# Stack loads with 4 KB rows, and the residual image in an SBUF ring of four

## The reference, cut to what matters

```python
x = x + _L0_conv_ref(_gn(x), ...)      # gn, router, shared conv, 2 expert convs, group norms, silu
x = x + _L1_conv_ref(_gn(x), ...)      # window attention on the result
# inside _L1_conv_ref
qkv = einsum('oc,bchw->bohw', qkv_w, x) + qkv_b
scores = einsum('bhnd,bhmd->bhnm', q, k) / sqrt(HD) + bias
o = einsum('bhnm,bhmd->bhnd', softmax(scores), v)
pe = depthwise_conv7x7(v_img)
out = einsum('oc,bchw->bohw', proj_w, x_img + pe) + proj_b
```

## Time and profile before

| | |
|---|---|
| median of 3 runs | 871.91 us |
| the profiled execution: its time | 872.17 us |
| the profiled execution: its span | 870.4 us |
| PE busy | 674.7 us, 78% |
| DVE busy | 601.1 us, 69% |
| ACT busy | 450.8 us, 52% |
| moved by DMA | 145.29 MB |
| one step of the loop in its middle | 40.9 us |

### The profile page before, as it was taken

The page is one execution under the profiler, slowest core; times in us unless marked ns, Lnnn a source line. Parts: engine busy times, 40 slices in busy tenths (PEclk is TensorE's granted clock), DMA queues, the critical chain, the costliest instruction groups (busy, mean ns, idle before and its releaser), DMA issues.

```text
span 870.4 us, 18688 instructions
## 1 busy us (share of the span) xinstructions
PE 674.7 (78%) x6926; PEld 409.1 (47%) x6926; DVE 601.1 (69%) x1136; ACT 450.8 (52%) x746; POOL 185.9 (21%) x289
## 2 busy tenths in 40 slices
PE   5225829696979788797979697979796969788785
PEld 4212315464646454555545454646463647444321
DVE  4734456778778787869687777777777888532396
ACT  1114445565657474746565556656565655354321
POOL 3122042222223130404130312222221011000044
PEclk9987759697989898989989897979797979999999
DMA  8232553948575664759594939394956345587345
GB/s 344 105 120 67 178 149 94 197 120 203 131 188 152 168 191 142 189 156 192 142 208 137 219 102 220 110 215 123 209 128 167 108 130 156 183 275 248 121 183 203
DMA packets 92751, 145.29 MB, mean 167 GB/s; under 512 B 24691, under 2 KB 65782, under 8 KB 92662
## 3 DMA queue, kind: packets, MB, share of 16 engines
q1 hardware_dynamic: 66806, 100.90, 41.1%
q0 software_dynamic: 21248, 25.36, 14.3%
q10 hardware_dynamic: 4608, 17.86, 5.6%
HBM read 84.21 MB, written 51.41 MB: 156 GB/s over the span
## 4 chain that ended last, share of the span: by engine, by line
PE 50%; DVE 20%; issue 12%; DMA 11%; ACT 3%; POOL 2%; POOLq 1%; SPq 1%; DVEq 0%; ACTq 0%
PE g L1069 14%; PE g L1087 5%; PE g L1065 5%; PE pv L1152 4%; PE t L1137 4%; DVE xr L840 4%; PE s L1126 3%; DMA vt<-x 3%; PE s L1259 3%; DMA xs<-xn 3%; PE g L1170 2%; PE t L1259 2%; PE g L1097 2%; PE s L1122 2%; DMA xsh<-xs 2%
## 5 line engine op out<-in xcount | busy, mean ns | idle before, releaser
L525 ACT ACTIVATE y<-g 128x512 f32<-128x512 f32 x96 | 57.1, 597 | 192.2 <-PE g L1065 104.4
L1069 PE MATMUL g<-xsh,wsel 96*128 96x512 f32 x256 | 132.1, 645 | 16.1 <-DMA xsh<-xs 15.4
L810 DVE BATCH_NORM_STATS2 st<-y 128x6 f32<-128x512 f32 x96 | 66.3, 692 | 99.1 <-ACT y L525 99.1
L874 DVE TENSOR_REDUCE mx<-s 128x8 f32<-128x512 f32 x128 | 87.2, 681 | 28.6 <-PE s L1126 27.9
L878 DVE TENSOR_TENSOR less<-s,mx 128x512 f32<-128x512 f32 x128 | 88.5, 692 | 4.4
L1122 PE MATMUL s<-bias,ident 128*128 128x512 f16 x128 | 51.1, 399 | 51.7 <-DMA stack<-sk_d 51.7
L1137 PE MATMUL t<-ident,less 128*128 128x128 f32 x512 | 79.4, 278 | 15.1 <-ACT pt L596 15.1
L596 ACT ACTIVATE pt<-t 128x512 f32<-128x512 f32 x128 | 74.7, 596 | 24.6 <-PE t L1137 18.0
L1137 PEld LDWEIGHTS t<-ident,less 128*128 128x128 f32 x512 | 62.4, 145 | 49.8 <-issue 36.9
L1152 PE MATMUL pv<-vp,pt 128*64 128x34 f32 x2048 | 82.8, 227 | 3.0 <-DVE ot L892 2.6
L1069 PEld LDWEIGHTS g<-xsh,wsel 96*128 96x128 f32 x256 | 49.5, 207 | 72.8 <-issue 54.0
(11 more groups left out here) (159 smaller groups left out, 1176.5 us busy)
## 6 DMA issues: line engine op xcount, KB each, us to landing
xsh<-xs POOLq DMA_DIRECT2D x64, 210.0 KB, 7.3
stack<-sq_d SPq DMA_DIRECT2D x96, 128.0 KB, 5.2
stack<-sk_d SPq DMA_DIRECT2D x192, 64.0 KB, 5.2
xs<-xn ACTq DMA_DIRECT2D x16, 578.0 KB, 3.3
vt<-x SPq DMA_DIRECT2D x4, 2048.0 KB, 18.3
xin<-x POOLq DMA_DIRECT2D x16, 512.0 KB, 7.8
acc_d<-xr SPq DMA_DIRECT2D x16, 512.0 KB, 5.1
sq_d<-qhl SPq DMA_DIRECT2D x32, 256.0 KB, 2.1
```

The lines of the kernel that those rows point to most:

```text
L525: act.activation(y[:, k, h * HALF:(h + 1) * HALF], g[at][:, :], ACT.Identity).then_inc(g_free[at], 1)
L810: last = v.bn_stats(st[:, 2 * k + h, :], y[:, k, h * HALF:(h + 1) * HALF])
L874: v.tensor_reduce(mx[:, p % 2, :], scored, AX.X, ALU.max).then_inc(sem["s_max"], 1)
L1069: last = mm(g[at][:, :], wsel[:, k - 1, C * dy:C * dy + C], xsh[:, k - 1, dy + 16 * h:dy + 16 * h + 16, 0:W], start=(dy == 0), stop=(dy == 1))
```

## The change

The DRAM copies of q and k are laid out by half, then high and low, and the channels of q and k are permuted on the host so that the four channels that one partition takes are neighbours: one row of 4 KB. The loads of a half go from 3 + 6 to 4 + 4: for each parity one of 16 partitions (`high_rows`) and one of 32 partitions that takes high and low together (`both_rows`). The tiles `qs` and `ks` get the same order, as does the score matmul. The single `xr` and `x1` become `xr` with four slots; the projection is added in the slot; save_xr and load_x1 go; save_acc and load_acc stay for the first 12 images, and the last four never leave SBUF. `l1s` moves into `vn`.

```diff
-STACK = 16 * 9
+STACK = 16 * 8
+KEEP = 4
-        xr = sb("xr", [C, PIX])
-        x1 = sb("x1", [C, PIX])
+        xr = sb("xr", [C, KEEP, PIX])
-        acc = free[0:B]
+        acc = free[0:B - KEEP] + [xr[:, n, :] for n in range(KEEP)]
-        sq_d = nc.dram_tensor("sq_d", [2, C, PIX], F16).ap()
+        sq_d = nc.dram_tensor("sq_d", [2, 2, C, HALF], F16).ap()
+            def high_rows(src, half, a):
+                return src[half, 0].rearrange("(a c i) n -> a c (i n)", a=2, i=Q)[a]
+
+            def both_rows(src, half, a):
+                size = C * HALF
+                return bass.AP(src.tensor, 2 * half * size + a * size // 2, [[size, 2], [Q * HALF, HD], [1, Q * HALF]])
...
-                for part, t in enumerate((0, 1, 0)):
-                    sp.dma_start(qs[QD * part:QD * part + QD, :, cols],
-                                 sq_d[t, :, cols].rearrange("(i c) n -> c i n", i=Q)).then_inc(stacked[half], 16)
+                for a in range(2):
+                    dst = qs[3 * HD * a:3 * HD * (a + 1), half, :, :].rearrange("p i n -> p (i n)")
+                    sp.dma_start(dst[0:HD], high_rows(sq_d, half, a)).then_inc(stacked[half], 16)
+                    sp.dma_start(dst[HD:3 * HD], both_rows(sq_d, half, a)).then_inc(stacked[half], 16)
...
-                for part, t in enumerate((0, 0, 1)):
-                    for par in range(2):
-                        rows = QD * part + HD * par
-                        src = sk_d[t, :, cols].rearrange("(i a c) n -> a c i n", i=Q, a=2)
-                        sp.dma_start(ks[rows:rows + HD, :, par, cols], src[par]).then_inc(stacked[half], 16)
+                for a in range(2):
+                    dst = ks[3 * HD * a:3 * HD * (a + 1), half, a, :, :].rearrange("p i n -> p (i n)")
+                    sp.dma_start(dst[0:2 * HD], both_rows(sk_d, half, a)).then_inc(stacked[half], 16)
+                    sp.dma_start(dst[2 * HD:3 * HD], high_rows(sk_d, half, a)).then_inc(stacked[half], 16)
...
             def step(b, has1, has2, has3):
-                if b:
-                    load_x1(b - 1)
...
-                if b:
+                if 0 < b <= B - KEEP:
                     save_acc(b - 1)
...
-                if has2:
-                    save_xr(b + 2)
...
                 if c == 1:
-                    act.wait_ge(sem["acc_saved"], 16 * B)
+                    act.wait_ge(sem["acc_saved"], 16 * (B - KEEP))
+                    for h in range(2):
+                        wait_emptied(act, "pr", B - 1, h)
-                if c:
+                if 0 < c <= B - KEEP:
                     load_acc(c - 1)
...
                 if part == 0:
-                    if j:
-                        dve.wait_ge(sem["xr_saved"], 16 * j)
-                        dve.wait_ge(sem["xw_done"], j)
+                    if j >= KEEP:
+                        dve.wait_ge(sem["acc_saved"], 16 * (j - KEEP + 1))
```

More of the change, by code:

```diff
@@ L151, in program @@
         stack = sb("stack", [C, 3 * Q * PIX // 2])
-        qs = stack[:, 0:Q * PIX // 2].bitcast(F16).rearrange("p (i n) -> p i n", i=Q)
-        ks = stack[:, Q * PIX // 2:].bitcast(F16).rearrange("p (i a n) -> p i a n", i=Q, a=2)
+        qs = stack[:, 0:Q * PIX // 2].bitcast(F16).rearrange("p (h i n) -> p h i n", h=2, i=Q)
+        ks = stack[:, Q * PIX // 2:].bitcast(F16).rearrange("p (h a i n) -> p h a i n", h=2, a=2, i=Q)
         TAPS = 2 * 2 * DWK * QD
@@ L193, in program @@
         ri = sb("ri", [B, 8], U32)
-        l1s = sb("l1s", [3, C])
+        l1s = vn[0:3, 0:C]
         hb = o[:, 0:TABLE]
-        free = [y[:, n, :] for n in range(3)] + [xin[:, 0, :], xin[:, 1, :], xr[:, :], x1[:, :], xw[:, :], o[:, :]]
+        free = [y[:, n, :] for n in range(3)] + [xin[:, 0, :], xin[:, 1, :], xw[:, :], o[:, :]]
         free += [t[:, :, :].rearrange("p t n -> p (t n)").bitcast(F32) for t in (qhl, khl)]
@@ L261, in save_half @@
                     sp.wait_ge(stacked[half], STACK * j)
-                sp.dma_start(dst.rearrange("t c n -> c t n")[:, :, cols], src[:, :, cols]).then_inc(saved[half], 16)
+                sp.dma_start(dst[half].rearrange("t c n -> c t n"), src[:, :, cols]).then_inc(saved[half], 16)
             def save_q(j):
@@ L331, in save_acc @@
                     wait_emptied(sp, "pr", b, h)
-                sp.dma_start(image_acc(b), x1[:, :]).then_inc(sem["acc_saved"], 16)
+                sp.dma_start(acc_d[b], xr[:, b % KEEP, :]).then_inc(sem["acc_saved"], 16)
             def step(b, has1, has2, has3):
-                if b:
-                    load_x1(b - 1)
                 if has1:
@@ L834, in residual @@
                 wk = [route[:, j, k:k + 1] for k in range(TOP)]
+                kept = xr[:, j % KEEP, :]
                 if part == 0:
                     dve.wait_ge(sem["silu_done"], 3 * j + 1)
-                    if j:
-                        dve.wait_ge(sem["xr_saved"], 16 * j)
-                        dve.wait_ge(sem["xw_done"], j)
-                    v.tensor_tensor(xr[:, :], y[:, 0, :], xin[:, j % 2, :], ALU.add).then_inc(sem["sum_shared"], 1)
+                    if j >= KEEP:
+                        dve.wait_ge(sem["acc_saved"], 16 * (j - KEEP + 1))
+                    v.tensor_tensor(kept, y[:, 0, :], xin[:, j % 2, :], ALU.add).then_inc(sem["sum_shared"], 1)
                     return
@@ L844, in residual @@
                     dve.wait_ge(sem["sum_shared"], j + 1)
-                    v.scalar_tensor_tensor(out=xr[:, :], in0=y[:, 1, :], scalar=wk[0], in1=xr[:, :],
+                    v.scalar_tensor_tensor(out=kept, in0=y[:, 1, :], scalar=wk[0], in1=kept,
                                            op0=ALU.mult, op1=ALU.add).then_inc(sem["sum_first"], 1)
@@ L849, in residual @@
                 dve.wait_ge(sem["sum_first"], j + 1)
-                v.scalar_tensor_tensor(out=xr[:, :], in0=y[:, 2, :], scalar=wk[1], in1=xr[:, :],
+                v.scalar_tensor_tensor(out=kept, in0=y[:, 2, :], scalar=wk[1], in1=kept,
                                        op0=ALU.mult, op1=ALU.add).then_inc(sem["xr_done"], 1)
@@ L853, in residual @@
                 for h in range(2):
-                    last = v.bn_stats(st[:, h, :], xr[:, h * HALF:(h + 1) * HALF])
+                    last = v.bn_stats(st[:, h, :], kept[:, h * HALF:(h + 1) * HALF])
                 last.then_inc(sem["bn_done"], 1)
@@ L906, in add_projection @@
             def add_projection(b, h):
-                dve.wait_ge(sem["x1_loaded"], 16 * b + 16)
+                dve.wait_ge(sem["xw_done"], b + 1)
+                dve.wait_ge(sem["xr_done"], b + 1)
                 at = wait_ready(dve, "pr", b, h)
                 part = slice(h * HALF, (h + 1) * HALF)
-                v.scalar_tensor_tensor(out=x1[:, part], in0=g[at][:, :], scalar=btot[:, 0:1], in1=x1[:, part],
+                v.scalar_tensor_tensor(out=xr[:, b % KEEP, part], in0=g[at][:, :], scalar=btot[:, 0:1], in1=xr[:, b % KEEP, part],
                                        op0=ALU.add, op1=ALU.add).then_inc(g_free[at], 1)
@@ L1124, in scores @@
                     for n in range(2):
-                        at = (2 * p + n) * TOK
-                        last = mm(bk[TOK * n:TOK * n + TOK, C * i:C * i + C], qs[0:3 * QD, i, at:at + TOK],
-                                  ks[0:3 * QD, i, :, at:at + TOK], start=False, stop=(i == Q - 1), skip_group_check=True)
+                        half, at = p // (PAIRS // 2), (2 * p + n) % PAIRS * TOK
+                        last = mm(bk[TOK * n:TOK * n + TOK, C * i:C * i + C], qs[0:3 * QD, half, i, at:at + TOK],
+                                  ks[0:3 * QD, half, :, i, at:at + TOK], start=False, stop=(i == Q - 1), skip_group_check=True)
                 last.then_inc(sem["s_ready"], 1)
@@ L1282, in _lay_out @@
     rw = a["L0_conv_router_w"]
-    cols = [qkv[0:C].T, qkv[C:2 * C].T, qkv[2 * C:].T, a["L1_conv_proj_w"].T, shared, rw[:, 0:C].T, rw[:, C:].T,
+    order = np.arange(C).reshape(Q, QD).T.reshape(-1)
+    cols = [qkv[0:C].T[:, order], qkv[C:2 * C].T[:, order], qkv[2 * C:].T, a["L1_conv_proj_w"].T, shared, rw[:, 0:C].T, rw[:, C:].T,
             a["L1_conv_cpb_w2"].T, a["L0_conv_expert_g"].T, a["L0_conv_expert_b"].T]
-    cols += [v.reshape(C, 1) for v in (a["L0_conv_gn_shared_g"], a["L0_conv_gn_shared_b"], a["L1_conv_qkv_b"][0:C],
-                                      a["L1_conv_qkv_b"][C:2 * C], a["L1_conv_qkv_b"][2 * C:], a["L1_conv_proj_b"])]
+    cols += [v.reshape(C, 1) for v in (a["L0_conv_gn_shared_g"], a["L0_conv_gn_shared_b"], a["L1_conv_qkv_b"][0:C][order],
+                                      a["L1_conv_qkv_b"][C:2 * C][order], a["L1_conv_qkv_b"][2 * C:], a["L1_conv_proj_b"])]
     turned = a["L1_conv_proj_w"].T.reshape(2, 2, CP, 2, C)
```

28 lines of the change are left out of this document (6 added, 22 removed).

## The result

The changed kernel takes 960.0 us (median of 4 runs, 955.3 to 961.8) against 871.8 us: ratio 1.0995, 95% interval 1.094 to 1.105. It is 88 us slower. The sign of the forecast (910 us) and its cause, stack loads on two DMA engines, hold; its size does not, and the time lies outside the range of 868 to 950. The medians of e8 and e11 each hold one slow run of four, which their ratios leave out.

A forecast was written before the change was run, and what follows sets the result against it. DVE's statistics were taken to set the step's end, behind PE's stack wait. 872.2 + 37.2 (half 0's delay) + 1 (clock) + 2 (setup) - 1 (depthwise part) = 911, stated as 910 us; range 868 to 950.

The forecast's parts named there:

- What bounds the kernel: In the loop, PE waits 4.0 us a step for the stack, then 1.44 for DVE's statistics; DVE sets the end.
- cover: PE's second wait, for DVE's statistics, absorbs a later stack up to 1.44 us a step; only the excess is paid.
- The ring: Residual slots replacing stores and reloads: 0 in the loop, including DVE's new wait for the acc store.
- both_rows on two engines: Stack loads whose source leads with size 2 run on 2 of the 16 DMA engines, always the same two.
- Rival A: Stack loads use all 16 engines, the stack lands earlier, DVE's statistics take over: 868 us (864 to 871), chance 0.14.
- The rate of an engine: One DMA engine moves 26 GB/s at best, so 64 KB of a both_rows load takes 2.5 us.
- The delay of half 0: Half 0 of k lands 4.3 us later (bounds 1.9 and 9.1); less cover, 2.9 us a step, 37.2 in 13.
- q's backlog: q's loads still unfinished on the two engines when half 0's k loads are issued: 2.2 us.
- The lower clock: Late scores run more often at the lower of two clocks: 1 us in all, bounds 0 and 5.
- The last steps: The step at 705 us has no stack wait and 6.11 us of cover, so it costs 0.
- The setup and the end: First image's loads delay the xsh loads PE awaits: +2 us (0 to 5); fewer depthwise loads: -1 (0 to -3.0).
- Rival C: Two engines' total load, including a sixteenth of other traffic, bounds the whole step: 945 us, chance 0.16.

The follow-up runs named there:

- e8: The changed kernel with k's loads cut into three of 16 rows, q's 32-row loads still leading with 2: 902.2 us, ratio 1.035.
- e11: The kernel before with only POOL's xsh loads led by their 16 channels instead of by 3: 864.3 us, ratio 0.987.
- e12: The changed kernel (ring of four) with stack loads led by 16 channels and xsh loads led by 16: 859.3 us, ratio 0.984.
- e2: The changed kernel with the stack loads, DRAM layout and channel order of the kernel before, so the ring of four alone: 869.0 us, ratio 0.997.
- e1: The changed kernel with its 32-partition loads led by the 16 channels, high/low second, same number of loads and bytes: 868.6 us, ratio 0.9946.
- e10: The changed kernel with POOL's xsh loads led by their 16 channels instead of by 3, wx rows reordered to match: 924.5 us, ratio 1.058.
- e4: The kernel before with the new 4 KB-row stack loads led by 16 channels, no ring: 870.0 us, ratio 0.9983.
- e6: The changed kernel with SP issuing half 0's q loads only after half 0's k save has landed: 975.2 us, ratio 1.117.
- e9: The changed kernel with POOL issuing a step's xin load only after half 0 of the stack has landed: 938.3 us, ratio 1.075.
- e13: The changed kernel with xsh loads led by 16 channels and xin issued after half 0 has landed: 912.0 us, ratio 1.043.
- e7: The changed kernel with q's loads cut into three of 16 rows, k's 32-row loads still leading with 2: 913.3 us, ratio 1.044.

## Why the prediction was right or wrong

**What bounds the kernel: right.** The two waits of PE behind one another, the second set by DVE, and a cover of 1.44 us a step. e11 and e12 show it from the other side: 49 us of stack wait could be taken away without shortening a steady step.

**The ring: right.** 0 in the loop (e2), and no wait of DVE for the acc store shows in the changed kernel.

**both_rows on two engines: right.** The packet count came out to the packet, the share is 0.13, and e1 undoes the slowdown by the order in which the same number of loads, of the same bytes and rows, walk their source. Rival A's time (868 us for 16 engines) is what e1 gave, 868.6.

The Trainium skill's rule on the number of engines ("DMA: Bandwidth & Descriptors", section on why a DMA increments its semaphore by 16) agrees with these rows on SP's queue for a leading 2, and with e10's on POOL's queue for a leading 3 against 16. The line of the Trainium skill on 512 B as enough for full rate (same page, "Specifications") is not borne out to the letter: packets of 1 KB on SP's queue took 46 ns and those of 4 KB 159 ns (medians, e2), which is 22 and 26 GB/s. The times of e1 and e4 can't test it, since DVE set the end of their steps.

The DMA share in the stretch of the k loads fell as forecast, to 0.47 between 400.71 and 414.25 us. Of their time to landing, which was to grow to 7 us or more, the profile of the changed kernel gives nothing.

**The rate of an engine: right.** 25.5 GB/s against 26.

**The delay of half 0: mis-sized, and this is the miss.** The term was "(5.3 - 1.9 - 1.2) + (5.3 - 3.2) = 4.3 us", a cost of 2.9 us a step. By the table PE's start came 38.2 us after the previous turn and now comes 45.1 after it: a delay of 6.9 us, and, less the cover, a step that is 5.6 longer, 73.6 us in 13 steps where the sum had 37.2. Two steps of the argument failed.

The first is q's backlog of 2.2 us when the k loads are issued. It was worked out from "the 208 GB/s of its stretch" and from an idle 15%. But the 208 GB/s were the bytes of every transfer in that stretch, the save and POOL's loads too, and the 15% were a share over 16 engines. The runs show that the head start is worth nearly nothing: 28 of 96 rows begun by then, and e6, which takes most of the head start away, leaves the time from the k loads' issue to PE's start at 14.8 us. With 68 of 96 rows still to come the backlog is some 3.8 us of the 5.3, an estimate from that count.

The second is xin. I had said that POOL's loads "pass over the same two engines" and took that only as a reason to stay off the lower bound; in the sum they have no term. Holding xin takes 1.5 us off the time from issue to PE's start, 1.7 us a step in the median time (e9), and the place of its issue (0.2 to 2.6 us ahead of PE's start) leaves the kernel before little of this to pay. The estimate of 1.6 more for q and the 1.5 of e9 make 7.4 us, near the 6.9 measured. That xin held in the kernel before would gain nothing was not run.

The xsh loads are not a missing term, though e10 gains 35.5 us by spreading them. They lengthen k's save, and they did so in the kernel before (8.1 us there, 4.1 in e11), where DVE's statistics hid it. The k loads of e10 and e13 take as long as those of the changed kernel. (Part of that may be q's, which has less head start when the save lands sooner; by e6 it is little.) So e13's 912 us beside the sum's 911 is luck: its k loads are issued 2.3 us earlier than before and take 6.0 longer, where the sum had 0 and 4.3.

e7 and e8 split the delay. Against the kernel before, PE's start comes 4.2 us later after the turn with k alone on two engines, and 2.5 later with q alone (38.2, 42.4 and 40.7 us); the forecast had 2.1 and 2.2. These are readings of single profiled executions, one 5 us over and one 9 us under its median, so that q's share is read low. Why k's part is twice its price is not settled.

**The lower clock: too small.** I took 1 us, with bounds of 0 and 5. Over the 12 steps of the table PE's busy time grew from 419.8 to 425.8 us with the same 3602 matmuls, at a mean granted clock of 0.90 before and 0.83 now, and by another 4.0 us in the last two steps (0.92 and 0.88). After the longer wait the clock stays at half speed longer: 0.50 in the first 4 us and 0.84 in the next 4 (from 414.25 us), where the kernel before had 0.51 and 1.00 (from 331.00 us). Together that is 10 us.

**The last steps: wrong.** I gave them 0 because of the 6.11 us of cover in the earlier trace rows. They cost 9.6 us, 4.0 of it in PE's busy time. In the step of the earlier trace rows the cover held, but the step after, which I did not count, loads the last image's stack too, and PE waits 6.48 us for it at 816.41, where no convolution stands beside it.

**The setup and the end: too small both.** 5.5 us for 2 up to the first turn, and -5.5 for -1; they cancel. In the setup PE's wait for xsh grew from 7.12 to 11.84 us, which is the place that the forecast named. The gain at the end is within the spread of that part, 110.7 to 117.8 us in the four profiled kernels without the ring and 105.4 to 116.2 in the eleven with it, so that how much of it is the ring's is not shown.

**Rival C** (945 us) was nearest in time, and for a reason near to the right one: the two engines carry the share of other transfers too. But it was not their total that bound. From 380 to 385 us, ahead of the next saves, the share is down to 0.02 (row below, changed kernel), and it is 0.03 or less for 4 us in each of 13 steps: they have a pause in every step. The bound is the chain from the k save to half 0.

```profile
380.00:385.00 5.00, 5.00 (x53) 2.83 (x51) 2.88 (x5) 2.58 (x7) 0.00 (x0) 1.00 0.02 5
```

**The range** failed because the upper bound of the delay (9.1 us, less the cover 7.7 us in 13 steps, 972 us) was worked out and then not held in it. The 2.2 us "to report" in its lower bound stand on no row.

## What to carry to other kernels

Write the outermost dimension of a DMA's source and destination so that 16 engines share it, and count the small packets or look for a DMA share of k sixteenths: a leading 2 or 3 is invisible in the bytes and in the mean GB/s. Price such a load on its own engines, with all other queues' traffic that crosses them, not on the mean over 16. Ask which transfers will fall into the longer wait that did not fall into the shorter one, as xin did. Remember that such a load can slow other transfers that have a piece on the same engines: the xsh loads doubled the landing time of a save in the kernel before. A wait with another close behind it is worth the difference, not itself. And when a version lands on the forecast's total, compare the parts before you take it for a proof.

## What the runs showed of the hardware that was not expected

- A load from POOL that leads with 3 leaves 208 more packets under 512 B than one that leads with 16 (832 for four loads in 50 to 66 us, none when they lead with 16). 208 is 13 x 16, the number of engines without data times the rows of each of the others, but no view says on which engines they are. On SP's queue a leading 2 leaves none: there the load reports from two engines only (21747, to the packet).
- POOL's loads that lead with 3 raised the landing of a 16-engine save on SP's queue from 4.0 to 7.6 us (e10 against the changed kernel), and from 4.1 to 8.1 in the kernel before (e11).
- Where two queues have work on the same two engines they share them about evenly: 13 packets of POOL's and 12 of SP's in the 2 us from 364.
- Packets of 1 KB took 46 ns and packets of 4 KB 159 ns (medians on SP's queue, e2): 22 against 26 GB/s for an engine.
